# Self attention of a fused transformer block: the exponentials taken group by group on ScalarE, with a scaled negative maximum as bias and the sums accumulated there

## The reference, cut to what matters

```
q = ln(fp8_linear(ln_out, wq)).reshape(b, s, 8, 2, 128)    # b = 16, s = 64: 8 groups, 2 heads each
k = ln(fp8_linear(ln_out, wk)); v = fp8_linear(ln_out, wv)
scores = einsum('bsghd,btgd->bghst', q, k) / sqrt(128)
p = softmax(scores, axis=-1)                               # over 64 keys
core = einsum('bghst,btgd->bsghd', p, v)
catq = fp8(clip(concat([core, xout]) / proj_smooth))       # xout: cross attention to 1601 context rows
```

## Time and profile before

| | us |
|---|---|
| median of 3 runs | 2562.75 |
| the profiled execution | 2561.66 |
| its span | 2559.8 |
| VectorE busy | 1937.3 (76%) |
| ScalarE busy | 1561.3 (61%) |
| TensorE matmul busy | 2266.5 (89%) |
| self attention by tiles, from the first maximum to the end | from 99.24 to about 382 |

### The profile page before, as it was taken

How to read it: one execution, slowest core, us unless ns; L and a number is a source line. 1 busy time by engine, 2 the same in 40 slices (tenths; PEclk the granted TensorE clock), 3 DMA queues, 4 the chain that set the end, 5 groups by cost and what they waited for, 6 DMA issues and landing times. The chain is left out here.

```text
span 2559.8 us, 49662 instructions
## 1 busy us (share of the span) xinstructions
PE 2266.5 (89%) x18258; PEld 1853.3 (72%) x18258; DVE 1937.3 (76%) x4402; ACT 1561.3 (61%) x3135; POOL 1405.7 (55%) x1537
## 2 busy tenths in 40 slices
PE   3868867999999999999999999999999999584666
PEld 1545656888888888888888888888888887362334
DVE  8988866777877777787777778777877877478753
ACT  5666645676777677677767767776776676211211
POOL 4334347776667677666767766676776655050000
PEclk8778879999999999999999999999999999786788
DMA  3112111101110111111011111101111000362100
GB/s 115 59 51 76 50 70 48 41 34 48 35 35 32 43 37 34 48 35 35 29 47 37 34 47 36 35 27 48 37 34 41 17 2 1 123 232 53 37 13 8
DMA packets 74478, 119.40 MB, mean 47 GB/s; under 512 B 21168, under 2 KB 56576, under 8 KB 73216
## 3 DMA queue, kind: packets, MB, share of 16 engines
q1 hardware_dynamic: 74240, 116.23, 13.4%
HBM read 94.20 MB, written 22.02 MB: 45 GB/s over the span
## 5 line engine op out<-in xcount | busy, mean ns | idle before, releaser
L75 PE MATMUL x_kc<-x_wk,x_ctxT 128*128 128x256 f16 x4992 | 623.3, 274 | 11.3 <-ACT x_sq L911 11.3
L75 PE MATMUL x_ox<-x_ctxp,x_pt 128*128 128x256 f16 x4992 | 609.6, 273 | 0.0
L681 POOL TENSOR_SCALAR x_kT<-x_kf 128x512 f16<-128x512 f32 (+1 forms) x448 | 282.2, 630 | 502.8 <-ACT x_kf L919 502.6
L75 PEld LDWEIGHTS x_kc<-x_wk,x_ctxT 128*128 128x128 f16 x4992 | 489.8, 98 | 82.7 <-ACT x_sq L911 14.5
L75 PEld LDWEIGHTS x_ox<-x_ctxp,x_pt 128*128 128x128 f16 x4992 | 484.3, 98 | 52.8
L683 POOL TENSOR_TENSOR x_kT<-x_kf,x_kT 128x512 f16<-128x512 f32 (+1 forms) x448 | 492.1, 1098 | 37.5
L1376 DVE TENSOR_TENSOR x_pt<-x_tp,x_pt 128x512 f16<-128x512 f32 (+1 forms) x512 | 288.9, 585 | 221.9 <-ACT x_pt L948 221.9
L1319 DVE TENSOR_REDUCE x_ss<-x_sq 128x4 f32<-128x512 f32 (+1 forms) x448 | 283.1, 644 | 170.1 <-ACT x_sq L911 169.6
L919 ACT ACTIVATE x_kf<-x_tp,x_hv 128x512 f32<-128x512 f32 (+1 forms) x448 | 331.8, 759 | 113.5 <-PE x_tp L1089 113.5
L907 ACT ACTIVATE x_kraw<-x_kc 128x512 f32<-128x512 f32 (+1 forms) x448 | 255.1, 569 | 150.8 <-PE x_kc L75 146.5
L948 ACT ACTIVATE x_pt<-x_tp 128x512 f16<-128x512 f32 (+1 forms) x512 | 259.3, 520 | 72.8 <-PE x_tp L1129 68.7
(11 more groups left out here) (246 smaller groups left out, 3048.4 us busy)
## 6 DMA issues: line engine op xcount, KB each, us to landing
x_stage<-in_ctxT SPq DMA_DIRECT2D x32, 800.5 KB, 4.4
x_stage<-in_ctx SPq DMA_DIRECT2D x16, 896.0 KB, 5.1
x_stage<-in_ctx SPq DMA_DIRECT2D x16, 640.0 KB
scr_q<-a_qxT SPq DMA_DIRECT2D x8, 1024.0 KB, 3.9
x_qs<-scr_q SPq DMA_DIRECT2D x16, 512.0 KB, 5.3
scr_core<-a_catc SPq DMA_DIRECT2D x8, 512.0 KB, 2.6
scr_x<-x_catx SPq DMA_DIRECT2D x8, 512.0 KB, 2.9
f_area<-in_wprojT SPq DMA_DIRECT2D x4, 1024.0 KB, 10.9
```

The lines of the kernel that those rows point to most:

```text
L75: last = pe.matmul(out, lhs[i], rhs[j], start=start and n == 0, stop=stop and n == len(parts) - 1)
L681: gp.tensor_scalar(dst[0], src, 1.0, 0.0, ALU.mult, ALU.add).then_inc(khi_ready, 1)
```

## The change

VectorE still takes the maximum, but then only multiplies the 8 maxima of a half by the negative softmax scale. ScalarE reads the scores out of PSUM and takes 8 exponentials of 64 columns for each half, each with its own bias and an accumulated sum. The subtraction and the sum on VectorE go. The banks of the scores count as free when the exponentials are done, not when the subtraction is. GpSimd's waits go over to the maximum's semaphore. A wait of VectorE for the stored core moves from ahead of the outputs to ahead of the buffer that needs it, and the counting of chained operations for each tile is replaced by one running count.

```diff
-            sem_, value = {"s": (sub_ready, t * 2), "t": (turned, (t + 1) * HU), "p": (pt_ready, t * 4),
+            sem_, value = {"s": (exp_ready, t * 2), "t": (turned, (t + 1) * HU), "p": (pt_ready, t * 4),
...
                 if 2 <= t < 4:
-                    gp.wait_ge(sub_ready, 2 * t + 2)
+                    gp.wait_ge(max_ready, 2 * t + 2)
...
             def exps(t, j):
-                act.wait_ge(sub_ready, t * 2 + j + 1)
-                act.activation(sm[:, 8 * j:8 * j + 8, :], sm[:, 8 * j:8 * j + 8, :], ACT.Exp,
-                               scale=SOFTMAX_SCALE).then_inc(exp_ready, 1)
+                act.wait_ge(max_ready, t * 2 + j + 1)
+                for i in range(8 * j, 8 * j + 8):
+                    src = tr[:, bank_of(("s", j)), (i - 8 * j) * S:(i - 8 * j + 1) * S]
+                    ins = act.activation(sm[:, i, :], src, ACT.Exp, bias=mx[:, i:i + 1], scale=SOFTMAX_SCALE,
+                                         accum_out=sums[:, i:i + 1])
+                ins.then_inc(exp_ready, 1)
...
                     c.done(v.tensor_reduce(mx[:, 8 * j:8 * j + 8], src, X, ALU.max))
-                    v.tensor_tensor(sm[:, 8 * j:8 * j + 8, :], src, mx[:, 8 * j:8 * j + 8].unsqueeze(2).to_broadcast([P, 8, S]),
-                                    ALU.subtract).then_inc(sub_ready, 1)
+                    v.tensor_scalar(mx[:, 8 * j:8 * j + 8], mx[:, 8 * j:8 * j + 8], -SOFTMAX_SCALE, None, ALU.mult
+                                    ).then_inc(max_ready, 1)
...
                     v.wait_ge(exp_ready, t * 2 + j + 1)
-                    e = sm[:, 8 * j:8 * j + 8, :]
-                    c.done(v.tensor_reduce(mx[:, 8 * j:8 * j + 8], e, X, ALU.add))
-                    c.done(v.reciprocal(mx[:, 8 * j:8 * j + 8], mx[:, 8 * j:8 * j + 8]))
+                    c.done(v.reciprocal(sums[:, 8 * j:8 * j + 8], sums[:, 8 * j:8 * j + 8]))
...
-                if not (isinstance(t, int) and t == 0):
-                    v.wait_ge(core_ready, t)
-                    v.sem_inc(passed_dve, 1)
...
-                    quantise(c, 0, 2048).then_inc(core_rounded, 1)
+                    rounding_steps(c, slice(0, 2048), core_ready, t)
+                    v.tensor_tensor(mg[:], yf[:], yb[:], ALU.add).then_inc(core_rounded, 1)
```

More of the change, by code:

```diff
@@ L139, in attend_self_and_cross @@
         mx = sb("mx", [P, 2 * G])
+        sums = sb("sums", [P, 2 * G])
         pr = early.enter_context(nc.psum_tensor("a_pr", [P, 4, 512], F32))
@@ L172, in attend_self_and_cross @@
         exp_ready = sem("exp_ready")
-        sub_ready = sem("sub_ready")
+        max_ready = sem("max_ready")
         probs_ready = sem("probs_ready")
@@ L277, in attend_self_and_cross @@
                      ("t", 6), ("t", 7), ("e", 4), ("e", 5), ("e", 6), ("e", 7), ("t", 8), ("t", 9), ("e", 8), ("e", 9)]
-        ATTEND_OPS = 9
-        DVE_PER_TILE = ATTEND_OPS + 16
         def weights(part, k, lo, hi):
@@ L1231, in _, with rounding_steps @@
             c.done(v.reciprocal(smooth[:], smooth[:]))
-            def quantise(c, at, n, kept=None):
-                at = slice(at, at + n)
+            def rounding_steps(c, at, kept, count):
                 c.done(v.tensor_scalar(yb[:, at], ys[:, at], FP8_MAX, -FP8_MAX, ALU.min, ALU.max))
                 c.done(v.tensor_scalar(eb[:, at], yb[:, at].bitcast(U16), 0x7F80, None, ALU.bitwise_and))
-                if kept is not None:
-                    v.wait_ge(xq_ready, kept)
+                if count:
+                    v.wait_ge(kept, count)
                 c.done(v.tensor_scalar(yf[:, at], eb[:, at].bitcast(BF16), FP8_MIN_NORMAL, FP8_ROUND, ALU.max, ALU.mult))
-                return v.tensor_tensor(mg[:, at], yf[:, at], yb[:, at], ALU.add)
             def low_weights(n0, n1):
@@ L1257, in rounding @@
                     v.wait_ge(y_scaled, KC * m + k + 1)
-                    quantise(c, k * T, T, KC * (m - 1) + k + 1 if m else None).then_inc(mg_ready, 1)
+                    at = slice(k * T, k * T + T)
+                    rounding_steps(c, at, xq_ready, KC * (m - 1) + k + 1 if m else 0)
+                    v.tensor_tensor(mg[:, at], yf[:, at], yb[:, at], ALU.add).then_inc(mg_ready, 1)
             low_weights(0, 2)
@@ L1445, in attend @@
                                               sm[:, 8 * j + b:8 * j + 8:2, :],
-                                              mx[:, 8 * j + b:8 * j + 8:2].unsqueeze(2).to_broadcast([P, 4, S]), ALU.mult)
+                                              sums[:, 8 * j + b:8 * j + 8:2].unsqueeze(2).to_broadcast([P, 4, S]), ALU.mult)
                     ins.then_inc(probs_ready, 1)
@@ L1477, in _ @@
             normalise(1, c, range(HU))
+            c = Chain(v, dve, 0, 0)
             def tile(t, more):
-                c = Chain(v, dve, DVE_PER_TILE, t)
                 attend(t, c)
@@ L1485, in tile @@
                     normalise(t + 2, c, range(4, HU))
-                    c.end()
             tile(0, True)
@@ L1490, in _ @@
                 tile(t, True)
[L1492 to L1495, removed]
+            tile(TILES - 2, False)
+            tile(TILES - 1, False)
             v.wait_ge(y_ready, TILES * 4)
+            v.wait_ge(core_ready, TILES - 1)
             c.done(v.tensor_scalar(yb[:], ys[:], FP8_MAX, -FP8_MAX, ALU.min, ALU.max))
```

## The result

The changed kernel takes 2567.68 us (median of 10 runs, 2566.20 to 2569.11), the kernel before beside it 2561.31 us (10 runs, 2560.01 to 2563.22): ratio 1.0025 (95% interval 1.0017 to 1.0032). It is slower by 6.4 us. The profiled executions have spans of 2566.0 and 2559.8 us, 6.2 apart, so they can be compared line by line.

The account below looks back on a forecast made before the run. A chain through ScalarE and TensorE, not VectorE, was taken to bound each tile's first part. Delays of 14.8 us (tiles 0 to 5), 3.3 (tile 6) and 3.1 (tile 7) sum to 21.2: 2584.0 us, range 2570 to 2602.

Parts of the forecast that it names:

- the work taken off VectorE: Ahead of VectorE's idle time in each tile: 2.7 us of subtractions and sums go, gain nothing save in the last tile.
- the second part of the tiles: From the third bank of moments to the next tile's maximum: set by VectorE's own work, as long as before.
- same: Whole kernel: 2557.6 to 2567.9 us can't be told from no change; chance 6%, against 90% slower and 4% faster.
- The pitch: ScalarE's 16 exponentials of 64 columns with accumulator reads: 0.34 us each, 5.44 us a tile.
- free reads: ScalarE's exponentials: accumulator reads free in a row, pitch 0.24 us, 12.8 us less, about 2571; chance 5%.
- The failed step: First part of tiles 0 to 5: e2 at +11.7, moments at +14.4 us, 2.7 us later in tiles 0, 1 and 4.
- the clock rival: TensorE's clock returns only within the outputs; t4, t5 and half the outputs at half speed, 16 us, about 2600; chance 14%.
- The idle time ahead of the third bank: VectorE's wait before the third bank of moments in a tile: grows from 3.0 us to 4 or more.
- None of it comes back later: Behind the stage: the 21.2 us delay arrives whole, since GpSimd starts there after 22.10 us of waiting for ScalarE's keys.
- Tile 6's own step: Tile 6, keys evacuated behind ScalarE's exponentials: 3.4 us late, nearly all passed on, taken as 3.3 us.
- tile 7's behind the exponentials: Tile 7, keys behind ScalarE's exponentials: 4.4 us late, less 1.4 for VectorE's sums, 3.1 us with the probabilities' bit.
- taken up behind the stage: Start of the cross attention: other waits make good some 17 us of the late start, about 2567; chance 4%.

Follow-up runs that it names:

- The doubled exponentials: Changed kernel with a second 64-column exponential without sum, its result overwritten, behind each of the 16: 2594.16 us, ratio 1.0125 to the kernel before.
- e2: Not a run: a unit of projection matmuls on TensorE in tiles 0 to 5, whose evacuation frees VectorE; in tile 0 of the changed kernel at +10.91 us.
- The pair with the clock held up: Kernel before and changed kernel, each with added matmuls (results overwritten) in TensorE's pauses in tiles 0 to 5: 2553.36 us and 2564.76 us.

## Why the prediction was wrong

*Right.* The chain through ScalarE sets the end, the work taken off VectorE is worth nothing there (in tile 2 its busy time fell by 2.8 us and its idle time grew by 2.1), the second part of the tiles stays as it was but for 0.7 us in tile 1, and the direction. By the forecast's own bounds, though, 2567.68 is "same" (2557.6 to 2567.9), to which it gave 6%. The doubled exponentials show the step from ScalarE's time to the tile's at one to one. 

*The pitch, mis-sized.* I took 0.34 us from the cross attention's 65-column form; it is 0.29 here. Heads t0 were forecast at +6.7 and came at +5.78, p2 at +10.0 and came at +9.15. In six tiles this is 0.85 x 6 = 5.1 us of the difference, in eight 16 x 0.05 x 8 = 6.4. The "free reads" rival is refuted: a read costs 0.093 us.

*The failed step* is "e2 is 1.73 behind p2 in tile 0 ... so +11.7, and the moments are at +14.4", with the 2.68 us "behind e2's start": distances measured at 1.2 GHz, carried over to a time at which the clock is 2.4. I had argued, against the clock rival, that TensorE "starts on p2 and goes on without a pause from there, as it does now, so the return should move with e2". It did not: the clock came back at about +11.2, e2 at +10.91. The moments came 1.95 us behind e2, at +12.86 in tile 0, and the outputs gained 7.1 us over the six tiles. The idle time ahead of the third bank, forecast at 4 us or more, was 2.80 to 3.64. The forecast also put the stretch behind the third bank down to VectorE alone; in tiles 0, 2, 3 and 4 of the kernel before VectorE waits another 0.48, 0.39, 0.51 and 0.83 us for the fourth bank, so a faster TensorE shortens it too. I had considered the clock only as something that could get worse. The pair with the clock held up, with tile 7's difference added back, gives 15.6 us, and the forecast's 21.2 less the 6.4 of the pitch is 14.8: so apart from pitch and clock the steps hold to within what that sum is good for.

*"None of it comes back later"* was wrong too: 4.5 us came back in tile 7, whose scores, values and keys ran at full clock in place of half. GpSimd's 22.10 us of waiting, which I read as proof that the delay would arrive whole, is 20.20 us after. Tile 6's own step was right (its outputs are 2.90 us later by its first maximum; forecast 3.3), tile 7's behind the exponentials about so (3.63 − 0.98 = 2.65; forecast 3.1).

*The sum.* Up to p2 9.4 us, tile 6 2.9, tile 7 2.65, tile 1's second part 0.7: 15.6. Given back: 7.1 before the outputs, 4.5 in tile 7's scores, keys and values, and 0.4 between tile 6's outputs and those scores. That leaves 3.6 us at the stage's end. 2.6 us are lost behind it. The rival "taken up behind the stage" named 2567 us, which is the time measured, but its mechanism isn't what happened: the time came back inside the stage, and behind it more was lost.

## What to carry to other kernels

A distance between two units of TensorE is read together with the granted clock over it, and can't be moved to another place without asking which clock it will meet there; a delay upstream can turn into less time downstream. `accum_out` on short rows isn't free: for 64 columns the read adds half of the exponential's own pitch, so with ScalarE on the chain one VectorE sum over many groups is better. Where TensorE waits in a pause among thin units, move real matmuls from behind into the pause: here a swap in two order lists gave 14.2 us, twice what the whole change cost.

## What the runs showed of the hardware

Behind an exponential of 64 columns the read of the accumulator costs 0.093 us of ScalarE's time (durations of 0.19 to 0.25 us overlap with the neighbours), and 64-column exponentials out of PSUM with a bias follow each other in 0.196 us without it. The same 32 matmuls of tile 7's scores took 7.06, 5.15, 4.85, 4.11, 4.08, 3.84 or 3.76 us in kernels that differ only upstream, as the clock stood when they came (0.50 over the 7.06 us, 0.98 over the 3.84). Between the kernel before and the changed one this is 3.2 us, half of the effect that was to be measured, so a change of a few us in this kernel can't be priced from one term of the chain alone.
